# A Mamba mixer's chunk states: fp32r products in three passes, two head pairs at a time

## The reference, cut to what matters

```
hBC = silu(causal_conv(proj))            # hid, B, C
hc = hid * dt                            # by chunk
states = einsum('bclhn,bhcl,bclhp->bchpn', B, exp(A_cs[-1] - A_cs), hc)
prev_states = scan of states over the chunks with exp(sum of A)
Y = (C B^T * L) hc + C prev_states * exp(A_cs)
out = residual + out_proj(rmsnorm((Y + D hid) * silu(gate)))
```

## Time and profile before

| | us |
|---|---|
| three runs, median | 1974.84 |
| lowest and highest | 1973.62, 1977.21 |
| span of the profiled execution | 1976.0 |

### The profile page before, as it was taken

The page is one execution under the profiler, slowest core; times in us unless marked ns, Lnnn a source line. Parts: engine busy times, 40 slices in busy tenths (PEclk is TensorE's granted clock), DMA queues, the critical chain, the costliest instruction groups (busy, mean ns, idle before and its releaser), DMA issues.

```text
span 1976.0 us, 33151 instructions
## 1 busy us (share of the span) xinstructions
PE 1932.9 (98%) x10858; PEld 1565.9 (79%) x10858; DVE 1558.0 (79%) x2867; ACT 1552.2 (79%) x3106; POOL 1386.6 (70%) x976
## 2 busy tenths in 40 slices
PE   8997899999999999999999999999999999999998
PEld 6573667778888888888888888888888888888876
DVE  8786899867777778787777787777777778787878
ACT  5363766658888888888989897979798888888886
POOL 5643577646777777777777777767676767777787
PEclk9999999999999999999999999999999999999999
DMA  5613323453343433343333333333343434343333
GB/s 206 197 65 117 107 90 103 143 197 99 118 124 111 125 118 122 115 122 118 111 123 105 125 104 128 113 115 126 103 136 105 130 106 131 102 164 113 116 117 123
DMA packets 114475, 241.76 MB, mean 122 GB/s; under 512 B 23681, under 2 KB 24706, under 8 KB 113794
## 3 DMA queue, kind: packets, MB, share of 16 engines
q1 hardware_dynamic: 110466, 227.06, 36.2%
q0 software_dynamic: 3840, 12.59, 2.1%
HBM read 226.75 MB, written 12.85 MB: 121 GB/s over the span
## 4 chain that ended last, share of the span: by engine, by line
PE 76%; DVE 2%; ACT 1%; issue 1%; DVEq 0%
PE ps L75 19%; PE ps L77 19%; PE ps L76 19%; PE ps L2117 6%; PE ps L2081 4%; PE ps L2125 4%; PE ps L2073 3%; PE ps L2057 1%; PE ps L2065 0%; PE ps L2107 0%; DVE s_y_lo L2502 0%; DVE s_cv L2410 0%; ACT s_lm L2200 0%; DVE s_end_g L2666 0%; ACT s_scale L2215 0%
## 5 line engine op out<-in xcount | busy, mean ns | idle before, releaser
L2677 POOL TENSOR_TENSOR w_lo<-w_raw,w_hi 128x1024 fp32r<-128x1024 f32 x142 | 338.1, 2390 | 217.3 <-ACT w_hi L2183 217.3
L75 PE MATMUL ps<-h_hi,w_hi 128*128 128x512 f32 x1168 | 469.8, 402 | 4.8 <-issue 1.6
L76 PE MATMUL ps<-h_lo,w_hi 128*128 128x512 f32 x1168 | 455.9, 390 | 0.0
L77 PE MATMUL ps<-h_hi,w_lo 128*128 128x512 f32 x1152 | 450.8, 391 | 0.0
L2410 DVE SCALAR_TENSOR_TENSOR s_cv<-ps,s_par,s_cv 128x511 f32<-128x511 f32 (+2 forms) x480 | 358.9, 748 | 114.1 <-ACT s_cv L2225 103.3
L2694 POOL TENSOR_TENSOR s_lm<-s_lm,s_cbt 128x512 f32<-128x512 f32 x256 | 328.3, 1306 | 121.8 <-ACT s_lm L2207 121.7
L2200 ACT ACTIVATE s_lm<-s_rows,s_steps 128x128 f32<-128x128 f32 x1024 | 318.5, 389 | 34.4 <-PE ps L2117 34.4
L75 PEld LDWEIGHTS ps<-h_hi,w_hi 128*128 128x128 f32 x1168 | 219.5, 188 | 53.8 <-DVE s_hid L2418 7.9
L77 PEld LDWEIGHTS ps<-h_hi,w_lo 128*128 128x128 f32 x1152 | 216.2, 188 | 46.9
L76 PEld LDWEIGHTS ps<-h_lo,w_hi 128*128 128x128 f32 x1168 | 219.9, 188 | 41.8 <-issue 0.2
L75 PE MATMUL ps<-s_wo_hi,s_y_hi 128*128 128x512 f32 x512 | 209.0, 408 | 1.8 <-DVE s_y_lo L2502 1.6
(11 more groups left out here) (327 smaller groups left out, 4246.0 us busy)
## 6 DMA issues: line engine op xcount, KB each, us to landing
w_raw<-in_w_in SPq DMA_DIRECT2D x144, 512.0 KB, 3.6
s_rows<-acs_dram SPq DMA_DIRECT2D x256, 256.0 KB, 3.7
s_wo_raw<-in_w_out SPq DMA_DIRECT2D x128, 256.0 KB, 3.2
w_raw<-in_gu_q SPq DMA_DIRECT2D x14, 512.0 KB, 3.6
f_d_q<-in_d_q SPq DMA_DIRECT2D x28, 256.0 KB, 2.7
f_d_w<-in_d_s SPq DMA_DIRECT2D x28, 256.0 KB, 3.5
table<-shifted SPq DMA_DIRECT2D x16, 256.0 KB, 2.5
xs<-in_x SPq DMA_DIRECT2D x8, 256.0 KB, 6.2
```

The lines of the kernel that those rows point to most:

```text
L75: nc.tensor.matmul(dst, l_hi, r_hi, start=start, stop=False)
L76: nc.tensor.matmul(dst, l_hi, r_lo, start=False, stop=False)
L77: return nc.tensor.matmul(dst, l_lo, r_hi, start=False, stop=stop)
L2677: nc.gpsimd.tensor_tensor(w_lo[:, slot, :], w_raw[:, slot, :], w_hi[:, slot, :].bitcast(F32), ALU.subtract).then_inc(w_lo_ready, 1)
```

## The change

ST is made for both pairs of a double by one set of products: for each of the three chunks one three-pass fp32r product of 256 columns (both pairs side by side), the first two chunks in bank C, the third in bank D. Its operands hdd and B get high halves from ScalarE (`act_hdd`, `act_b`) and low halves from GpSimd (`pool_hdd`, `pool_b`). The last unit keeps the native product by pair. OP is cut in two halves of two tiles, OP_1 and OP_2, and ST stands between the halves of OP a (in double 1 ahead of OP a). SQ moves to bank A. VectorE's state is done for both pairs at once when both products are done: in doubles 1 to 3 behind the tile b, in double 0 between silu a and tile b. ScalarE's tap of b moves between the two differences of pair b. B's transpose is kept once, not twice, end_g takes the place of an earlier buffer, and some semaphores are merged.

```diff
 def double_jobs(s):
...
+    both = [(C_BANK, ("ST", *divmod(a + 2, KC))), (D_BANK, ("ST", *divmod(b + 2, KC)))]
+    one, two = (None, ("OP_1", 0, a)), (None, ("OP_2", 0, a))
     if s == 1:
-        jobs += [(None, ("OP", 0, a)), (B_BANK, ("H", 1, B_AT)), second]
...
+        jobs += [*both, one, two, (B_BANK, ("H", 1, B_AT))]
     else:
+        if s == 2:
+            jobs += [(A_BANK, ("CB", 1, 0))]
+        if s == 3:
+            jobs += [(A_BANK, ("SQ", 0, 0))]
+        jobs += [one, *both, two]
+    return jobs + [(None, ("OP_1", 0, b)), (None, ("OP_2", 0, b))]
...
+        hdd_hi, hdd_lo = [sb(f"s_hdd_{part}", [P, TB - 1, 2, P], F32R) for part in ("hi", "lo")]
+        hdd = sb("s_hdd", [P, TB - 1, 2, P])
...
-        end_g = sb("s_end_g", [P, TB, D])
+        end_g = weights.stage
...
         def pe_state(pe, v, k, dst):
+            pe.wait_ge(state_lo_ready, v.at(KC + 1, (k | 1) + 1))
+            for at, i in enumerate((2,) if k % 2 else (0, 1)):
+                mm = three_passes(nc, dst[:, at * 2 * P:(at + 1) * 2 * P], b_hi[:, i, :], b_lo[:, i, :],
+                                  hdd_hi[:, i].rearrange("p e c -> p (e c)"), hdd_lo[:, i].rearrange("p e c -> p (e c)"),
+                                  True, True)
+            mm.then_inc(done["ST"], 1)
...
+        def act_hdd(act, v, k):
+            act.wait_ge(took["T"], v.at(KC, k))
+            nc.scalar.activation(hdd_hi[:, :, k % 2, :], hdd[:, :, k % 2, :], ACT.Copy).then_inc(state_hi_ready, 1)
+
+        def act_b(act, v):
+            act.wait_ge(took["BT"], v.at(1, 0))
+            nc.scalar.activation(b_hi[:], b_l[:], ACT.Copy).then_inc(state_hi_ready, 1)
...
         def act_double(act, un, s):
...
             act_exps(act, ua, a_on)
+            if s == 3:
+                act_b(act, v)
+            act_hdd(act, ua, a_on)
             act_gate(act, v, b, bank(un, ("G", 1, b)))
             if s:
                 act_tanh(act, v, tile_of(a), h_a)
+            act_hdd(act, ub, b_on)
             act_diff(act, ub, 2 * b_on)
+            act_tap(act, v, tile_of(b), h_b)
             act_diff(act, ub, 2 * b_on + 1)
-            act_tap(act, v, tile_of(b), h_b)
             if not s:
                 act_tanh(act, v, tile_of(a), h_a)
             act_exps(act, ub, b_on)
...
+        def dve_state(dve, v, k, one, two):
+            base = (v.u * KC + k) * 2
+            dve.wait_ge(done["ST"], v.at(KC, k + 1))
+            if not (v.first and k == 0):
+                dve.wait_ge(done["OFF"], v.u * KC + k)
+            nc.vector.tensor_copy(state[:, :, 0, :], one[:, 0:2 * P].rearrange("p (e c) -> p e c", e=2)
+                                  ).then_inc(state_chain, 2)
+            for e in range(2):
+                dve.wait_ge(state_chain, base + 2)
+                dve_state_step(v, k + e, 1, one[:, (2 + e) * P:(3 + e) * P]).then_inc(state_chain, 1)
+            for e in range(2):
+                dve.wait_ge(state_chain, base + 3 + e)
+                dve_state_step(v, k + e, 2, two[:, e * P:(e + 1) * P]).then_inc(took["ST"], 1)
...
         def dve_double(dve, un, s):
...
             if s == 0:
                 dve_tile(dve, v, tile_of(a), h[0])
-                state(0)
                 dve_silu(dve, v, tile_of(a), h[0])
-                state(1)
+                state()
                 dve_tile(dve, v, tile_of(b), h[1])
                 dve_silu(dve, v, tile_of(b), h[1])
             elif s == 1:
...
                 dve_tile(dve, v, tile_of(b), h[1])
-                state(0)
+                state()
                 dve_silu(dve, v, tile_of(b), h[1])
...
+            else:
+                if s == 3:
+                    dve_ssq(dve, un, bank(un, ("SQ", 0, 0)))
                 dve_tile(dve, v, tile_of(b), h[1])
-                state(1)
+                state()
+                if s == 2:
+                    dve_cb(dve, v, bank(un, ("CB", 1, 0)))
                 dve_silu(dve, v, tile_of(b), h[1])
...
+        def pool_hdd(pool, v, k):
+            pool.wait_ge(state_hi_ready, v.at(KC + 1, k + 1))
+            nc.gpsimd.tensor_tensor(hdd_lo[:, :, k % 2, :], hdd[:, :, k % 2, :], hdd_hi[:, :, k % 2, :].bitcast(F32),
+                                    ALU.subtract).then_inc(state_lo_ready, 1)
...
         def pool_double(pool, un, s):
...
             pool_sum(pool, un, b)
             if s == 1:
                 pool_w(pool, v, LOADS.index(("BC", 0)))
+            if s == 3:
+                pool_b(pool, v)
+            pool_hdd(pool, *pair_at(un, a + 2))
+            pool_hdd(pool, *pair_at(un, b + 2))
             pool_m(pool, *pair_at(un, a + 2))
             pool_m(pool, *pair_at(un, b + 2))
```

More of the change, by code:

```diff
@@ L1719, in last_jobs @@
         if k:
-            jobs += [(None, ("OP", 0, k - 1))]
+            jobs += [(None, ("OP_1", 0, k - 1)), (None, ("OP_2", 0, k - 1))]
         if k + 2 < KC:
@@ L1861, in bank_free @@
                     u = (un.u if owner is un else un.u - 1) + ahead
-                    pe.wait_ge(freed[kind], u * TURNS[kind] + i + 1)
+                    last = i | 1 if kind == "ST" and not (owner.scans and owner.last) else i
+                    pe.wait_ge(freed[kind], u * TURNS[kind] + last + 1)
                     return
@@ L1953, in sp_params @@
             if wait is not None:
-                sp.wait_ge(y_hi_ready, wait)
+                sp.wait_ge(y_hi_ready, 2 * wait)
                 sp.wait_ge(y_lo_ready, wait)
@@ L2080, in pe_state @@
             for i in range(TB - 1):
-                mm = nc.tensor.matmul(dst[:, i * P:(i + 1) * P], b_l[:, v.b, i, :], hdd[:, k % 2, i, :],
-                                      start=True, stop=True)
+                mm = nc.tensor.matmul(dst[:, i * P:(i + 1) * P], b_l[:, i, :], hdd[:, i, k % 2, :], start=True, stop=True)
             mm.then_inc(done["ST"], 1)
@@ L2133, in pe_unit @@
                 v = un.ahead(n)
-                if kind == "OP":
-                    for at in (0, 2):
-                        if i == 0 and not un.first:
-                            pe.wait_ge(op_took, (un.u - 1) * TB + at + 2)
-                        pe_op(pe, un, i, (at, at + 1))
+                if kind in ("OP_1", "OP_2"):
+                    tile = 0 if kind == "OP_1" else 2
+                    if i == 0 and not un.first:
+                        pe.wait_ge(op_took, (un.u - 1) * TB + tile + 2)
+                    pe_op(pe, un, i, (tile, tile + 1))
                     continue
@@ L2147, in pe_unit @@
                     pe_ssq(pe, v, dst)
+                elif kind == "ST" and un.scans and un.last:
+                    pe_state_alone(pe, v, i, dst)
                 elif kind == "ST":
@@ L2371, in act_end, with dve_state_alone @@
             act_rms(act, un)
-        def dve_state(dve, v, k, src, c):
+        def dve_state_alone(dve, v, k, src, c):
             if c == 0:
                 dve.wait_ge(done["ST"], v.at(KC, k))
-                if k >= 2 or not v.first:
-                    dve.wait_ge(done["OFF"], v.u * KC + k - 1)
+                dve.wait_ge(done["OFF"], v.u * KC + k - 1)
                 nc.vector.tensor_copy(state[:, k % 2, 0, :], src[:, 0:P]).then_inc(state_chain, 1)
@@ L2551, in dve_first @@
                     dve_skip(dve, v)
-            dve_state(dve, v, 0, bank(un, ("ST", 1, 0)), 1)
-            dve_state(dve, v, 0, bank(un, ("ST", 1, 0)), 2)
-            for c in range(TB - 1):
-                dve_state(dve, v, 1, bank(un, ("ST", 1, 1)), c)
+            dve_state(dve, v, 0, bank(un, ("ST", 1, 0)), bank(un, ("ST", 1, 1)))
             dve_tile(dve, *tile(KC - 1))
@@ L2564, in dve_double, with state @@
             h = [bank(un, ("H", 1, tile_of(k))) for k in (a, b)]
-            def state(i):
-                for c in range(TB - 1):
-                    dve_state(dve, *on[i][:3], c)
+            def state():
+                dve_state(dve, on[0][0], on[0][1], on[0][2], on[1][2])
             def turn(i):
```

88 lines of the change are left out of this document (40 added, 48 removed).

## The result

The changed kernel takes 2009.4 us (median of 4 runs, 2001.5 to 2010.5) against 1974.2 us (1967.5 to 1977.2) of the kernel before beside it: a ratio of 1.0168, with an interval of 1.0149 to 1.0188. It is slower, by some 33 us (0.0168 x 1974), where +19 us and 1994 us were forecast. The sign was forecast, the size was not, and 2009.4 lies above the range, 1959 to 2004.

A forecast was written before the change was run, and what follows sets the result against it. TensorE was taken to bound the kernel (98% busy). Terms -0.25 + 1.0 + 0.6 - 0.25 + 0.4 = +1.5 us a unit, taken as 1.3, gave +19 us over 15 units: 1994 us, range 1959 to 2004.

The forecast's parts named there:

- TensorE's own work: ST of each double: nine fp32r passes at 0.12 us replace twelve native instructions, saving 0.25 us a double, 12 to 18 us.
- The sum of 1.5 a unit: Net of all four doubles of a unit, +1.5 us, taken as 1.3 for a possible saving between native and fp32r passes.
- What is added: Work beside TensorE in a double: ScalarE copies 0.45 us each, GpSimd subtractions 1.0 us each, VectorE's joint state 2.2 us.
- Double 3: Second hdd copy waits for VectorE's turn, so differences, last silu and second DIAG come 1.0 us later: net +1.0 us.
- swapping tap and difference shifts no sum: On ScalarE's queue in double 3, the changed order of tap and difference was claimed to add no time.
- Doubles 0 and 1: Up to the C projection +0.6 us a unit instead of -0.25; then ST gives 0.25 back and B projection waits 0.4 more.
- Double 2: GpSimd's second hdd half is ready 0.7 us before ST, VectorE's state 0.5 before OFF: net -0.25 us.
- The saving of 0.25 comes through: In double 2, TensorE's shorter ST was claimed to show fully, 0.25 us, as operands are ready for ST and OFF.
- The prologue: The prologue's one double was counted among the 61 doubles that each save 0.25 us of TensorE work.
- All hidden: Rival: hdd copies fit ScalarE's idle, last silu at most 0.25 us later, TensorE's 15 us come through: 1960 us; 24%.
- only the handoff: Rival: only double 3's handoff costs, +1.2 us wait against -1.0 work a unit: +3 us, 1978 us; 19%.
- GpSimd late: Rival: slower subtractions make ST wait another 0.5 to 0.8 us in two doubles, 10 us or more: 2005 us; 9%.
- Loads not hidden: Rival: weight loads exposed in ST, nine passes at 0.22 us, +0.64 us a double, 39 us in all: 2014 us; 2%.

The follow-up runs named there:

- the mended kernel: Changed kernel with CB behind ST, old taps except in double 1, pair b's high half by VectorE, silu a earlier in double 1: 1974.3 us, ratio 1.0025.

## Why the prediction was right or wrong

**TensorE's own work: right as a rate, wrong as a sum.** 0.12 us a pass, and 0.26 to 0.28 us a double in three of four, are measured where nothing else binds (double 0 gave 0.07). In the changed order four doubles give 0.60 instead of 1.0. Over 15 units that is 9 us, below the bound of 12. Even the 0.89 where less binds is 13 us, short of 15, since most of double 0's gain goes into what is left of the DIAG wait. The sum of 1.5 a unit was also lowered to 1.3 for a saving between native and fp32r passes that no row had shown; double 3 came out 0.31 shorter instead of 0.25, so there is little of it.

**"What is added": near.** The copy holds the queue for 0.41 to 0.43 us (0.45 forecast), a subtraction takes 1.02 (1.0), the state 2.07 (2.2).

**Double 3: right.** The copy waits for the turn, the differences go behind it, the DIAG wait is 1.20 (1.25 by the forecast's terms), 14 times, and the double itself is 0.31 shorter. But "swapping tap and difference shifts no sum" is wrong. The order of two instructions on a queue shifts no sum as long as neither waits; the tap does wait for TensorE, 0.62 us in double 3 when no copy delays it. Beside the copies it cost nothing, as they had already eaten that time, and gained 0.77 in double 1; without splits it costs 1.27 us a unit.

**Doubles 0 and 1: near in size, partly for other reasons.** The DIAG wait and these two together were forecast at 1.25 + 0.6 - 0.25 + 0.4 = 2.0 and measured at 0.96 + 0.69 = 1.65. The B projection starts 0.47 us behind the pass before it (1101.38 to 1101.85), 0.24 more than a pass takes, where 0.4 was forecast. The C projection is late, and GpSimd's low half of the B/C weights is named ahead of it, as forecast. But the earlier trace rows had named the silu of a as what the C projection waited for, which the prediction passed over, and the rows of the kernel after show that it is nearly as late as the weights:

```profile
1092.39 2.41 POOL L2710 TENSOR_TENSOR w_lo<-w_raw,w_hi 128x1024 fp32r<-128x1024 f32 x1
...
1094.05 0.69 DVE L2465 SCALAR_TENSOR_TENSOR s_hid<-ps,s_cv 128x512 f32<-128x512 f32 x1
...
1094.94 0.47 PE L75 MATMUL ps<-h_hi,w_hi 128*128 128x512 f32 x1 [0.57 <-POOL w_lo L2710]
```

They end at 1094.80 and 1094.74. Taking the first away gave 0.12 us on the mended kernel, where the projections then waited for a silu.

**Double 2: the step that failed.** "The saving of 0.25 comes through" looked at ST's operands and at OFF's, and not at what was moved ahead of ST. The change puts CB there, into a bank that the silu of a has yet to free; it waits 0.61 us in each of 15 units. The double is 0.54 longer instead of 0.25 shorter, and CB's place alone measures 0.87 us a unit, 13 us in the mixer. With CB put back behind ST the same double is 0.31 shorter, so the reading of ST's and OFF's operands was right and the moved job was what it left out. The diff and the table of banks had it: a moved job brings its bank's wait with it.

**The prologue: the other step that failed.** It was counted as one of 61 doubles that gain 0.25. It has none of their cover: GpSimd gets B and two hdd halves behind a weight. ST waits 3.54 us, TensorE runs at half clock until 463.4, and the stretch is 4.15 us longer. Without any split it is 55.13, what it was before. The miss of some 14 us is 7.4 in the 15 units (26.9 against 15 x 1.3 = 19.5), 4.15 here and 2.1 in the last unit, which the sum left at nothing.

**The rivals.** "All hidden" and "only the handoff" fell with the DIAG wait of 16.7 us and the growth of double 1. "GpSimd late" named the nearest total, 2005, and that is luck: leaving its subtractions out moves no unit, though they are late once, in the prologue. "Loads not hidden" fell with the passes 0.12 us apart.

## What to carry to other kernels

When a change moves jobs in a hand-written order, list for every job moved, not only for the one rewritten, which bank or buffer it takes and who frees it when; CB, moved to make room and otherwise unchanged, cost 0.87 of the 1.88 us a unit here. An operation inserted in a full queue behind an operand that comes late pushes everything after it, whatever that engine's busy share, and two such causes on one handoff don't add: undoing one shows little, so test them two by two. Look at the prologue and the last unit apart: the one has the same new work and none of the cover, the other keeps shared helpers whose new work it doesn't need.

## What the runs showed of the hardware

- Three-pass fp32r products of 256 columns run at 0.12 us a pass, each with its own 128x128 weight load of 0.19 us beside it. Against native fp32 products of 128 columns that was worth 0.26 to 0.28 us in three doubles of four, out of 1.34.
- TensorE's granted clock fell to 0.50 in the prologue of some executions and not of others with the same wait: behind 3.16 us it stayed at 1.00 once and fell once, and so behind 1.51 us. At 0.50 nine 256-column passes took 2.06 us instead of 1.08, and a prologue 1.5 us more. Behind the DIAG waits of 1.2 us in the steady units no such loss is seen: the 512-column passes there are 0.23 us apart (1061.15 to 1061.38).
- CB's native products between fp32r passes took 0.81 us from start to start behind ST, and 0.92 behind a wait: 0.11 us beyond the wait itself.
